# A 16-bit output product, ScalarE norms and an x tile taken ahead in a Mamba sandwich kernel

## The chip, the cores and the metric

The kernel runs on one core of one Trainium2 chip, whose engines TensorE, VectorE, ScalarE, GpSimd and SyncE run side by side, each in the order of its own queue. The metric is the device time of one launch in microseconds (us), lower is better.

## The reference

The input is 8 batches of 1024 tokens by 256 features, all float32. Every batch passes a state-space layer and a feed-forward layer, each between a layer norm of its input and one of its output, with the input added:

```python
x = x + _layernorm(mamba(_layernorm(x)))
x = x + _layernorm(ffn(_layernorm(x)))
# mamba: INNER = 512, 8 heads of 64, state 64
x = silu(causal_conv(inp @ Wx.T))            # 4 taps
z = inp @ Wz.T
b, c = x @ Wb.T, x @ Wc.T                    # per head
dt = softplus(x @ Wdt.T + b_dt)
state = exp(dt * a) * state + (dt * b) outer x ;  y = c . state   # over tokens
y = y + d_param * x
yn = group norm of y per head, over ALL tokens and 64 channels
out = (yn * silu(z)) @ Wout.T
# ffn: 1024 hidden, weights alpha * sign(w), exact gelu
```

The group norm needs the sums over all 1024 tokens of a batch before any of its output can be normalised, gated and multiplied by Wout.

## The kernel before

**Tiles.** A batch is two blocks (j = 0, 1) of 512 tokens, a block four chunks (q) of 128 tokens. Channels lie on partitions for the x, z, B and C projections (four tiles c of 128 channels by 512 tokens), tokens on partitions for the norms, Wout and the last feed-forward product. Projections run as three f16 products of high and low halves (split_product, L1429); a low half is what rounding to f16 left (x_low L1076, hidden_split L1283). The Wout product (attention_out, L1594) is f32, four products of 256 columns for each 128 tokens, each seen as two records.

**Order of the work.** turn_steps writes one list of steps for a batch, by hand. Every engine walks the same list and does its own part of each step, strictly in that order. Steps of kind "own" belong to batch b, "tail" to batch b-1 (its group norm, Wout, middle norm, feed-forward and end norm), "next" to batch b+1. So the tail of one batch is woven into the next. opening_steps stands before the first batch, and last_tail holds the tail of the last one, which nothing covers.

A block goes: head (x projected, convolved over its taps on VectorE at L1071, silu, high and low halves; z; in block 0 the group norm's end and the gate, and the tail's Wout product), B, dt, middle norm, C with the feed-forward's hidden tiles, then the chunk stage. In it, chunk q has a front (segment exponentials on ScalarE, x and B turned by TensorE, x times dt on VectorE L1175, its weighted form on GpSimd L788), a score (TensorE L1541, masked by VectorE L1184), ends (the decays at the chunk's ends: TensorE L1530, ScalarE exponential L991, times C on GpSimd L795), a carry (state products L1555 and L1564; GpSimd scales the state L806, VectorE adds L1190) and a back (TensorE L1577, VectorE adds into y, L1200). Woven in are the tail's second output product (O), its end statistics and root, end_norm and end_add, and for the following block in_stat, in_norm and the two transposes xT.

The end of the chunk stage, in the list before:

```python
steps += own(("front", j, 2)) + tail(("end_stat", j))
steps += own(("score", j, 2), ("carry", j, 1), ("ends", j, 2)) + tail(("end_root", j)) + own(("back", j, 1), ("head_stat", j, 0))
steps += own(("front", j, 3), ("score", j, 3)) + [(who, "xT", nj, 0)] + tail(("end_norm", j, 0))
steps += own(("carry", j, 2), ("ends", j, 3), ("back", j, 2)) + [(who, "silu_table"), (who, "xT", nj, 1)] + tail(("end_norm", j, 1))
steps += own(("carry", j, 3), ("back", j, 3))
```

**Norms.** statistics (L1033 to L1040) runs on VectorE, the inverse root on GpSimd (L740), and the norm itself, (v - mean) * root, on VectorE (normal, L1046) for all four norms: in, mid, ff, end. The input norm writes xn, which TensorE turns at L1439.

**Banks.** PSUM's eight banks are three rings: five for "own" products, two for the tail's, one for xT, cums and sums. A product waits (empty) until the product that was five back in its ring has been read; the x projection's tiles 1, 2 and 3 so wait for the readers of the last chunk's state and y products. The group-norm mean is one small product (L1584), its root is on GpSimd (L746), and ScalarE normalises (L999) what VectorE (L1245, block 0) or GpSimd (L772, block 1) multiplies by the gate.

## Time and profile before

| what | value |
|---|---|
| median of 3 runs | 1340.73 us (1339.92 to 1341.39) |
| profiled execution | 1339.59 us |
| its span in the profile | 1337.9 us |
| TensorE busy | 1261.0 us (94%) |
| VectorE busy | 1053.6 us (79%) |
| ScalarE busy | 751.2 us (56%) |
| GpSimd busy | 450.9 us (34%) |
| mean busy share of the DMA engines, by hardware queue | 7.4% |

The span runs from the first instruction to the last. PE is TensorE, PEld its weight loads, DVE VectorE, ACT ScalarE, POOL GpSimd. A timeline row gives a start and a length in us from the span's start; the bracket is how long the engine was idle before it, and which instruction ended that. Back-to-back instructions overlap by up to 0.1 us in the records, so busy time over count says what one costs in a row.

### The profile page before, as it was taken

The page shows a single profiled execution, that of the slowest core. Times are in us where ns is not written, and L with a number is a line of the kernel's source. Part 1 is how long each engine was busy: PE and PEld are TensorE (multiplying, and loading weights), DVE is VectorE, ACT ScalarE, POOL GpSimd, SP SyncE. Part 2 cuts the span into 40 slices and gives each one's busy share as a digit, 9 for nine tenths or more (in the row PEclk, how much of TensorE's full clock was granted, in tenths as well). Part 3 has the DMA queues.
Part 4 walks back from the last instruction along what each step waited for, and adds up shares of the span by engine and source line. Part 5 has one row for each costly group of instructions (what it writes and reads, how often), then busy time and mean ns, then how long its engine had stood idle before and what let it go on. Part 6 is the DMA issues. An engine that isn't in the chain of part 4 may idle for free.

```text
span 1337.9 us, 27890 instructions
## 1 busy us (share of the span) xinstructions
PE 1261.0 (94%) x10616; PEld 810.2 (61%) x10616; DVE 1053.6 (79%) x2494; ACT 751.2 (56%) x1270; POOL 450.9 (34%) x527
## 2 busy tenths in 40 slices
PE   6898999999999999999999999999999999999775
PEld 3564657566565756656575665757566575766543
DVE  5585878879887897878888798878978789786675
ACT  5564674547654475555745567454856548455321
POOL 2030335133441533324342233514243153322523
PEclk9999999999999999999999999999999999999878
DMA  7010000101010010101001010000101000010000
GB/s 225 1 49 1 17 0 2 48 1 49 1 49 1 2 48 1 49 0 49 1 1 48 1 49 1 26 24 2 48 1 49 1 21 13 1 33 1 33 1 31
DMA packets 30564, 32.89 MB, mean 25 GB/s; under 512 B 1856, under 2 KB 28628, under 8 KB 30432
## 3 DMA queue, kind: packets, MB, share of 16 engines
q1 hardware_dynamic: 30432, 31.11, 7.4%
q8 instruction: 85, 1.39, 0.4%
q14 instruction: 47, 0.39, 0.1%
HBM read 22.72 MB, written 8.39 MB: 23 GB/s over the span
## 4 chain that ended last, share of the span: by engine, by line
PE 68%; DVE 22%; issue 4%; ACT 3%; POOL 3%; DVEq 0%; POOLq 0%; ACTq 0%
PE bank L1429 24%; PE bank L1622 8%; PE bank L1609 8%; DVE xs L1071 4%; PE bank L1594 4%; PE bank L1541 4%; PE bank L1577 4%; PE bank L1519 4%; PE bank L1511 3%; DVE un L1046 2%; PE bank L1439 2%; PE bank L1564 2%; PE bank L1555 2%; DVE stats_end L1033 2%; PE bank L1530 1%
## 5 line engine op out<-in xcount | busy, mean ns | idle before, releaser
L795 POOL TENSOR_TENSOR Cd<-Cd,CT 128x512 f32<-128x512 f32 x64 | 83.5, 1305 | 376.7 <-ACT Cd L991 376.7
L1429 PE MATMUL bank<-sh,WbT 128*128 128x512 f16 x768 | 174.7, 383 | 7.1 <-DVE sh L1076 7.1
L1429 PE MATMUL bank<-sh,WcT 128*128 128x512 f16 x768 | 175.9, 379 | 0.0
L1071 DVE SCALAR_TENSOR_TENSOR xs<-xi,vectors,xs 128x512 f32<-128x512 f32 x192 | 143.2, 750 | 17.6 <-ACT xs L898 13.3
L1429 PEld LDWEIGHTS bank<-sh,WbT 128*128 128x128 f16 x768 | 74.1, 98 | 94.9 <-DVE sh L1076 6.4
L981 ACT ACTIVATE mt<-bank 128x512 f32<-128x512 f32 x128 | 69.6, 599 | 108.0 <-PE bank L1511 108.0
L1594 PE MATMUL bank<-WoutT,yT 128*128 128x256 f32 x512 | 117.8, 387 | 11.8 <-DVE yT L1245 11.8
L1429 PEld LDWEIGHTS bank<-sh,WcT 128*128 128x128 f16 x768 | 75.0, 98 | 86.7
L1609 PE MATMUL bank<-uh,sign1T 128*128 128x512 f16 x512 | 122.9, 386 | 2.6 <-DVE uh L1272 2.6
L1013 ACT ACTIVATE hf<-bank,vectors,alpha 128x512 f32<-128x512 f32 x128 | 99.6, 778 | 40.1 <-PE bank L1609 29.3
L1622 PE MATMUL bank<-sign2T,hh 128*128 128x256 f16 x1024 | 119.4, 276 | 1.8 <-DVE hh L1283 1.8
L1594 PEld LDWEIGHTS bank<-WoutT,yT 128*128 128x128 f32 x512 | 97.6, 193 | 31.9 <-DVE yT L1245 18.2
L957 ACT ACTIVATE CT<-bank 128x512 f32<-128x512 f32 x64 | 38.1, 595 | 136.1 <-PE bank L1429 136.1
L1622 PEld LDWEIGHTS bank<-sign2T,hh 128*128 128x128 f16 x1024 | 99.9, 99 | 19.3 <-issue 4.3
L1281 DVE TENSOR_SCALAR hh<-hf 128x512 f16<-128x512 f32 x128 | 54.9, 429 | 59.0 <-ACT hf L1013 58.5
L1184 DVE TENSOR_TENSOR mt<-bank,mt 128x512 f32<-128x512 f32 x128 | 82.4, 685 | 14.3 <-PE bank L1541 13.8
L1283 DVE SCALAR_TENSOR_TENSOR hh<-hf,hh 128x512 f16<-128x512 f32 x128 | 88.6, 692 | 4.4
L740 POOL TENSOR_TENSOR rstd_mid<-var_eps_mid,power 128x4 f32<-128x4 f32 x16 | 16.2, 1013 | 222.9 <-DVE var_eps_mid L1040 222.9
L1429 PE MATMUL bank<-xh,WxT 128*128 128x512 f16 x384 | 88.6, 385 | 0.0
L991 ACT ACTIVATE Cd<-bank 128x512 f32<-128x512 f32 x64 | 38.2, 597 | 88.6 <-PE bank L1530 88.6
L1609 PEld LDWEIGHTS bank<-uh,sign1T 128*128 128x128 f16 x512 | 49.5, 99 | 62.0 <-issue 6.4
L1429 PE MATMUL bank<-xh,WzT 128*128 128x512 f16 x384 | 85.7, 379 | 0.0
(196 smaller groups left out, 2524.3 us busy)
## 6 DMA issues: line engine op xcount, KB each, us to landing
xt<-L_attn_input_tensor_dram SPq DMA_DIRECT2D x16, 512.0 KB, 5.1
u<-L_attn_input_tensor_dram SPq DMA_DIRECT2D x16, 512.0 KB, 4.0
out_dram<-u SPq DMA_DIRECT2D x16, 512.0 KB, 3.0
yT<-in_L_ffn_w_dram SPq DMA_DIRECT2D x2, 512.0 KB, 8.9
u<-in_L_ffn_w_dram SPq DMA_DIRECT2D x2, 512.0 KB, 9.2
BT<-in_L_attn_Wx_dram SPq DMA_DIRECT2D x1, 512.0 KB, 4.8
...
```

Of the source, the lines that this page charges most:

```text
L795: pool.tensor_tensor(Cd[n % 2][:, :, :], Cd[n % 2][:, :, :], CT[:, :, q * P:(q + 1) * P], ALU.mult)\
L981: nc.scalar.activation(mt[n % 2][:, g].rearrange("p c t -> p (c t)"), bank(t, ("seg", j, q, g))[:, :], ACT.Exp).then_inc(seg_exp.sem, 1)
L1013: nc.scalar.activation(hf[f % 2][:, :], bank(t, ("H", j, f))[:, :], ACT.Gelu, bias=b1_col[:, f:f + 1], scale=alpha1[:, f:f + 1]).then_inc( ...
L1071: nc.vector.scalar_tensor_tensor(out=xs[:, c, :], in0=xi[:, c, k:k + BLK], scalar=taps[:, c, k:k + 1], in1=xs[:, c, :], op0=ALU.mult, op1= ...
L1184: nc.vector.tensor_tensor(v, bank(t, ("S", j, q, g))[:, :], v, ALU.mult).then_inc(mt_out.sem, 1)
L1281: nc.vector.tensor_scalar(hh[0][:, f, :], hf[f % 2][:, :], SG, None, ALU.mult).then_inc(hh_hi.sem, 1)
L1283: nc.vector.scalar_tensor_tensor(out=hh[1][:, f, :], in0=hf[f % 2][:, :], scalar=SG, in1=hh[0][:, f, :], op0=ALU.mult, op1=ALU.subtract).t ...
L1429: mm = nc.tensor.matmul(bank(t, key)[:, :], w[i][:, k, cols(m)], v[h][:, k, :], start=(a == 0), stop=(a == len(terms) - 1))
L1519: mm = nc.tensor.transpose(bank(t, key)[:, cols(c)], src[:, c, cols(q)], ident[:, :])
L1594: mm = nc.tensor.matmul(bank(t, key)[:, (i % 2) * D:(i % 2 + 1) * D], yT[:, c, (j * NQ + i) * P:(j * NQ + i + 1) * P], WoutT[:, c, :], sta ...
L1609: mm = nc.tensor.matmul(bank(t, key)[:, :], sign1T[:, k, cols(f)], uh[i][:, k, :], start=(a == 0), stop=(a == len(terms) - 1))
L1622: mm = nc.tensor.matmul(bank(t, key)[:, (i % 2) * D:(i % 2 + 1) * D], hh[p][:, f, cols(i)], sign2T[:, f, :], start=(a == 0), stop=(a == le ...
```

## The change

- The Wout product of block 1 becomes three f16 products (high x high, low weight x high, high x low) of 256 columns. Its operands are made by ScalarE (gated_high) and VectorE (gated_low), in block 0's chunk stage, into the buffer of the feed-forward's hidden halves. The weight is split once. The statistics of the middle norm take an epsilon scaled alike.
- The input and the end norm move from VectorE to ScalarE, as Identity with a scale (the root) and a bias (minus mean times root, made by a tiny VectorE instruction, shift). The input norm is written over xt, and x of the next batch is loaded when TensorE has turned it. xn is gone.
- In the chunk stage both transposes of the next block's input, the end statistics, the end root and the head statistics get other places.
- In block 1's chunk stage the first x tile of the next batch is projected after the scores of chunk 3, in the ring of one bank, and convolved in a buffer of its own (ahead) between back 2 and carry 3; the silu is in the next head, whose order changes with it.

The diff's core, with its parts in their order:

```diff
@@ -163,10 +164,10 @@
             steps += own(("z_silu",))
         elif j == 0:
 
-            steps += own(("xi", 0, 0), ("xi", 0, 1), ("xi", 0, 2)) + tail(("head_stat", NJ - 1, 1), ("gn_sum",), ("gn_mean",))
-            steps += own(("xi", 0, 3), ("conv", 0, 0), ("silu", 0, 0), ("xs_hi", 0, 0)) + tail(("gn_root",))
-            steps += own(("conv", 0, 1, 0, 2), ("z", 0, 0)) + tail(("gn_fold",)) + own(("conv", 0, 1, 2, 3), ("z", 0, 1))
-            steps += tail(("gate", 0, 0)) + own(("xs", 0, 0), ("silu", 0, 1), ("xs_hi", 0, 1), ("conv", 0, 2))
+            steps += own(("silu", 0, 0), ("xs_hi", 0, 0), ("xi", 0, 1), ("xi", 0, 2), ("xi", 0, 3))
+            steps += tail(("head_stat", NJ - 1, 1), ("gn_sum",), ("gn_mean",)) + own(("conv", 0, 1, 0, 1)) + tail(("gn_root",))
+            steps += own(("conv", 0, 1, 1, 3), ("z", 0, 0)) + tail(("gn_fold",)) + own(("conv", 0, 2, 0, 1), ("z", 0, 1))
+            steps += tail(("gate", 0, 0)) + own(("xs", 0, 0), ("silu", 0, 1), ("xs_hi", 0, 1), ("conv", 0, 2, 1, 3))
             steps += own(("z", 0, 2), ("z", 0, 3)) + tail(("gate", 0, 1)) + own(("xs", 0, 1), ("conv", 0, 3))
             steps += tail(("Wo", 0, 0)) + own(*[("z_in", 0, c) for c in range(KI)])
             for c in (2, 3):
...
@@ -215,11 +216,15 @@
         steps += own(("score", j, 1))
         norm = [(who, "in_norm", nj)]
         steps += own(("carry", j, 0), ("ends", j, 1)) + (own(("back", j, 0)) + norm if first else norm + tail(("O", j, 1)) + own(("back", j, 0)))
-        steps += own(("front", j, 2)) + tail(("end_stat", j))
-        steps += own(("score", j, 2), ("carry", j, 1), ("ends", j, 2)) + tail(("end_root", j)) + own(("back", j, 1), ("head_stat", j, 0))
-        steps += own(("front", j, 3), ("score", j, 3)) + [(who, "xT", nj, 0)] + tail(("end_norm", j, 0))
-        steps += own(("carry", j, 2), ("ends", j, 3), ("back", j, 2)) + [(who, "silu_table"), (who, "xT", nj, 1)] + tail(("end_norm", j, 1))
-        steps += own(("carry", j, 3), ("back", j, 3))
+        steps += own(("front", j, 2)) + [(who, "xT", nj, 0)] + own(("score", j, 2), ("carry", j, 1), ("ends", j, 2))
+        steps += [(who, "xT", nj, 1)] + own(("back", j, 1)) + tail(("end_stat", j)) + own(("front", j, 3), ("score", j, 3)) + tail(("end_root", j))
+        steps += [(who, "xi", nj, 0)] if j else []
+        steps += own(("head_stat", 1, 0)) if j else []
+        steps += own(("carry", j, 2), ("ends", j, 3)) + tail(("end_norm", j, 0), ("end_norm", j, 1)) + own(("back", j, 2))
+        steps += tail(("gated", 1, 0)) if j == 0 else []
+        steps += [(who, "conv", nj, 0)] if j else []
+        steps += [(who, "silu_table")] + own(("carry", j, 3), ("back", j, 3)) + ([] if j else own(("head_stat", 0, 0)))
+        steps += tail(("gated", 1, 1)) if j == 0 else []
         if j == 0:
...
-    steps += [("Wo", 0, 0), ("Wo", 0, 1), ("mid_stat", 0), ("mid_norm", 0), ("ff_stat", 0), ("ff_norm", 0)]
+    steps += [("Wo", 0, 0), ("Wo", 0, 1), ("mid_stat", 0), ("gated", 1, 0), ("gated", 1, 1), ("mid_norm", 0), ("ff_stat", 0), ("ff_norm", 0)]
...
+        WoutT_parts = [sb(f"WoutT{i}", [P, KI, D], F16) for i in range(2)]
...
-        xn = sb("xn", [P, NQ, D])
...
+        yg = [[v[:, j * KI:(j + 1) * KI, :] for v in hh] for j in range(NJ)]
+        ahead = hh[1][:, 0:2, :].rearrange("p a n -> p (a n)").bitcast(F32)
...
-            (tail_keys if who == "tail" else in_keys if kind in ("xT", "cums", "sums") else own_keys).extend(uses(kind, *at))
-        in_keys.sort(key=lambda key: (key[1], ("xT", "cums", "sums").index(key[0]), key))
+            turned = kind in ("xT", "cums", "sums") or (kind, *at) == ("xi", 0, 0)
+            (tail_keys if who == "tail" else in_keys if turned else own_keys).extend(uses(kind, *at))
+        in_keys.sort(key=lambda key: (key[1], ("xT", "xi", "cums", "sums").index(key[0]), key))
...
+        def conv_sum(j, c):
+            return ahead if j == c == 0 else xs[:, c, :]
...
-                sp.wait_ge(*xn_made.count(t.ago(1), (j + 1) * NQ))
+                if not opening(t):
+                    sp.wait_ge(*full(t.ago(1), ("xT", j, KD - 1)))
...
+            def normal(w, v, t, j, i):
+                act.wait_ge(*ln_shifts[w].count(t, j + 1))
+                nc.scalar.activation(v[:, i, :], v[:, i, :], ACT.Identity, bias=ln_shift[w][:, i:i + 1],
+                                     scale=rstd[w][:, i:i + 1]).then_inc(normed[w].sem, 1)
+
+            def input_norm(t, j):
+                for i in range(NQ):
+                    normal("in", xt[j], t, j, i)
+
+            def end_norm(t, j, m=None):
+                for i in range(NQ) if m is None else range(2 * m, 2 * m + 2):
+                    normal("end", ffn_buffer(t, j), t, j, i)
...
-                if c == 0:
-
-                    act.wait_ge(*full(s, ("X", sj, NQ - 1)))
-                    act.wait_ge(*sh_lo.count(s, (sj + 1) * KI))
-                    act.wait_ge(*skip_out.count(s, (sj + 1) * KI))
-                nc.scalar.activation(xs[:, c, :], bank(t, ("xi", j, c))[:, :], ACT.Identity, bias=conv_bias[:, c:c + 1],
+                if j == c == 0:
+                    if not opening(t):
+                        act.wait_ge(*full(t.ago(2), ("O", NJ - 1, NQ // 2 - 1)))
+                elif c == (0 if j else 1):
+                    past_readers(t, j)
+                nc.scalar.activation(conv_sum(j, c), bank(t, ("xi", j, c))[:, :], ACT.Identity, bias=conv_bias[:, c:c + 1],
                                      scale=last_tap[:, c:c + 1]).then_inc(tap_out.sem, 1)
...
             def x_silu(t, j, c):
                 act.wait_ge(*conv_out.count(t, (j * KI + c + 1) * (TAPS - 1)))
-                nc.scalar.activation(xs[:, c, :], xs[:, c, :], ACT.Silu).then_inc(xs_out.sem, 1)
+                if j == c == 0:
+                    past_readers(t, j)
+                nc.scalar.activation(xs[:, c, :], conv_sum(j, c), ACT.Silu).then_inc(xs_out.sem, 1)
...
+            def gated_high(t, j, m):
+                s, sj = (t, 0) if ring_of(t, ("O", 0, 0)) is not final else (t.ago(1), NJ - 1)
+                act.wait_ge(*full(s, ("O", sj, NQ // 2 - 1)))
+                for c in range(2 * m, 2 * m + 2 if j else 0):
+                    act.wait_ge(*g_late.count(t, KI + c + 1))
+                    nc.scalar.activation(yg[j][0][:, c, :], yT[:, c, BLK:T], ACT.Copy, scale=SY).then_inc(yg_hi.sem, 1)
...
+            def shift(w):
+                def step(t, j, m=0):
+                    if m:
+                        return
+                    dve.wait_ge(*ln_rstd[w].count(t, j + 1))
+                    nc.vector.scalar_tensor_tensor(out=ln_shift[w][:, :], in0=moments[w][:, :, 0], scalar=-1.0,
+                                                   in1=rstd[w][:, :], op0=ALU.mult, op1=ALU.mult).then_inc(ln_shifts[w].sem, 1)
+                return step
...
+            def gated_low(t, j, m):
+                for c in range(2 * m, 2 * m + 2 if j else 0):
+                    dve.wait_ge(*yg_hi.count(t, c + 1))
+                    nc.vector.scalar_tensor_tensor(out=yg[j][1][:, c, :], in0=yT[:, c, BLK:T], scalar=SY, in1=yg[j][0][:, c, :],
+                                                   op0=ALU.mult, op1=ALU.subtract).then_inc(yg_lo.sem, 1)
...
+                    if t.b + t.d + 1 < NB:
+                        dve.wait_ge(*xs_out.count(t.ago(-1), j * KI + 1))
...
-                pe.wait_ge(*(g_late.count(t, (m + 1) * KI) if j else g_out.count(t, (m + 1) * KI)))
+                pe.wait_ge(*(yg_lo.count(t, KI) if j else g_out.count(t, (m + 1) * KI)))
                 pe.wait_ge(*empty(t, key))
-                for i in (2 * m, 2 * m + 1):
+                for i in (2 * m, 2 * m + 1) if j else ():
+                    terms = [(c, w, v) for c in range(KI) for w, v in ((0, 0), (1, 0), (0, 1))]
+                    for a, (c, w, v) in enumerate(terms):
+                        mm = nc.tensor.matmul(bank(t, key)[:, (i % 2) * D:(i % 2 + 1) * D], yg[j][v][:, c, cols(i)],
+                                              WoutT_parts[w][:, c, :], start=(a == 0), stop=(a == len(terms) - 1))
```

## Rows read from the trace of the kernel before

**Rows 1.** Windows, one batch: us, then busy time (records) of each engine, TensorE's clock.
```profile
604.00:761.36 157.36, 153.89 (x1325) 98.93 (x1321) 130.38 (x309) 92.42 (x156) 55.38 (x62) 1.00 0.07 21
```

**Rows 2.** Timeline, TensorE, block 1's chunks and next head: start, us, work [idle before <- releaser].
```profile
613.61 0.40 PE L1530 MATMUL bank<-of_target,end_mask 64*64 64x512 f16 x2 [0.68 <-DVE mt L1184]
...
617.48 0.66 PE L1439 MATMUL bank<-ident,xn 128*128 128x128 f32 x4
...
621.93 0.67 PE L1564 MATMUL bank<-Cd,state 64*64 64x128 f32 x16 [0.16 <-issue]
...
623.56 4.06 PE L1429 MATMUL bank<-xh,WxT 128*128 128x512 f16 x18
...
635.27 3.72 PE L1594 MATMUL bank<-WoutT,yT 128*128 128x256 f32 x16 [0.54 <-DVE yT L1245]
...
639.45 3.72 PE L1594 MATMUL bank<-WoutT,yT 128*128 128x256 f32 x16 [0.46 <-DVE yT L1245]
```

**Rows 3.** Timeline, TensorE, head of block 1.
```profile
703.82 5.35 PE L1429 MATMUL bank<-xh,WxT 128*128 128x512 f16 x24
...
714.19 7.07 PE L1594 MATMUL bank<-WoutT,yT 128*128 128x256 f32 x32
...
721.10 2.75 PE L1429 MATMUL bank<-sh,WbT 128*128 128x512 f16 x12
```

**Rows 4.** Timeline, VectorE, end statistics, middle statistics, convolutions and last low halves.
```profile
610.83 1.39 DVE L1033 BATCH_NORM_STATS2 stats_end<-y 128x6 f32<-128x256 f32 x4
...
644.20 1.42 DVE L1033 BATCH_NORM_STATS2 stats_mid<-bank 128x6 f32<-128x256 f32 x4
...
706.68 2.33 DVE L1071 SCALAR_TENSOR_TENSOR xs<-xi,vectors,xs 128x512 f32<-128x512 f32 x3 [1.23 <-ACT xs L898]
...
718.85 1.29 DVE L1076 SCALAR_TENSOR_TENSOR sh<-xs,sh 128x512 f16<-128x512 f32 x2 [0.62 <-ACT sh L931]
```

**Rows 5.** Groups of instructions by form: shapes, count | busy us, mean ns | idle before.
```profile
L1594 PE MATMUL bank<-WoutT,yT 128*128 128x256 f32 x512 | 117.8, 387 | 11.8 <-DVE yT L1245 11.8
...
L1622 PE MATMUL bank<-sign2T,hh 128*128 128x256 f16 x1024 | 119.4, 276 | 1.8 <-DVE hh L1283 1.8
...
L931 ACT ACTIVATE sh<-xs 128x512 f16<-128x512 f32 x64 | 39.1, 622 | 1.0
...
L1283 DVE SCALAR_TENSOR_TENSOR hh<-hf,hh 128x512 f16<-128x512 f32 x128 | 88.6, 692 | 4.4
...
L1046 DVE TENSOR_SCALAR y<-y,moments_end,rstd_end 128x256 f32<-128x256 f32 x60 | 36.7, 652 | 1.1 <-POOL rstd_end L740 1.1
...
L1046 DVE TENSOR_SCALAR xn<-xt,moments_in,rstd_in 128x256 f32<-128x256 f32 x64 | 32.3, 564 | 1.2 <-POOL rstd_in L740 1.2
...
L999 ACT ACTIVATE yT<-yT,gn_shift,gn_scale 128x256 f32<-128x256 f32 x128 | 65.1, 586 | 14.4 <-DVE gn_shift L1238 14.4
...
L1234 DVE TENSOR_TENSOR gn_scale<-gn_rstd,vectors 128x4 f32<-128x4 f32 x8 | 1.3, 162 | 2.0 <-POOL gn_rstd L746 1.1
...
L870 ACT ACT_TABLE_LOAD x30 | 38.5, 1283 | 0.5
```

**Rows 6.** Timeline, GpSimd: two group-norm roots, and chunks 2 and 3 of block 1.
```profile
473.23 1.47 POOL L746 TENSOR_TENSOR gn_rstd<-gn_var,power 128x4 f32<-128x4 f32 x1 [4.45 <-DVE gn_var L1229]
...
615.97 1.01 POOL L740 TENSOR_TENSOR rstd_end<-var_eps_end,power 128x4 f32<-128x4 f32 x1
...
617.64 1.04 POOL L788 TENSOR_TENSOR xdw<-xdt,decays 128x512 f32<-128x512 f32 x1 [0.66 <-DVE xdt L1175]
...
619.46 0.61 POOL L806 TENSOR_TENSOR state<-state,decays 128x256 f32<-128x256 f32 x1 [0.77 <-PE bank L1564]
...
620.26 1.41 POOL L795 TENSOR_TENSOR Cd<-Cd,CT 128x512 f32<-128x512 f32 x1 [0.19 <-ACT Cd L991]
...
630.60 1.47 POOL L746 TENSOR_TENSOR gn_rstd<-gn_var,power 128x4 f32<-128x4 f32 x1 [4.45 <-DVE gn_var L1229]
```

**Rows 7.** Timeline, VectorE, middle norm after the last batch.
```profile
1273.92 1.90 DVE L1046 TENSOR_SCALAR un<-bank,moments_mid,rstd_mid 128x256 f32<-128x256 f32 x4 [1.20 <-POOL rstd_mid L740]
```

68 lines of the change are left out of this document (39 added, 29 removed).

## The prediction

> **What bounds the kernel now.** I read the page first (TensorE 94% busy), then one batch by windows, then TensorE's timeline for its gaps, then the other engines' timelines beside those gaps. One batch lasts 157.37 us, from one group-norm root on GpSimd to the next (473.23 to 630.60) [rows 6], and in a stretch of that length TensorE works in all but 3.5 us [rows 1], at the full 2.4 GHz. The gaps sit in two places. In the chunk stage of either block TensorE waits 0.68 us for VectorE's masked scores before the ends of chunk 2, and 0.16 us for the decayed C of chunk 3 [rows 2]. In the head of block 0 it waits for the gated output before each half of the output product (0.54 and 0.46 us) [rows 2]. The head of block 1 has no gap: the two projections and the output product run through and the B projection follows [rows 3]. So TensorE is the bound, but VectorE's chain is close behind: its last low half in block 1 is ready at 720.14 us and B's last quarter wants it at 721.10 + 1.95 = 723.05 us, a slack of 2.9 us [rows 3, 4].
>
> **The 16-bit product.** Block 1's output product is 32 records of f32 now and becomes 48 of f16. The f32 ones take 117.8/512 = 0.230 us each, f16 ones of the same 256 columns 119.4/1024 = 0.117 us [rows 5]; by the stretch of block 1, 6.9 us become 48 x 0.109 = 5.2 us. TensorE is offered 1.7 us per batch, 13.8 us over eight. For it ScalarE makes four high halves (39.1/64 = 0.61 us each) and VectorE four low halves (0.69 us each) per batch [rows 5]. The Trainium skill, Perfetto Trace Analysis, Identifying the Most-Contended Engine, says to work on the engine with the highest occupancy first. By that rule the sum would be these 13.8 us and the time some 1326 us; the windows show whether the other engines let it through, and that is a rival below.
>
> **The norms.** VectorE loses eight end norms of 36.7/60 = 0.61 us and eight input norms of 0.50 us a batch, 8.9 us; it gains the four low halves, 2.8 us, and four tiny shifts of 0.16 us [rows 5]. ScalarE takes 16 norms at 65.1/128 = 0.51 us [rows 5], and has gaps for the input ones. The price beside other work is nothing; if ScalarE were late there, the transposes would be late by as much. x is loaded in place and freed by TensorE instead of VectorE, some 8 us later in SP's queue, tens of us before its use: nothing.
>
> **The chunk stage, both blocks.** I go through block 1's; block 0's is the same 80.26 us later.
> - End statistics leave the place before chunk 2's masked scores, so the 0.68 us gap goes; both transposes of x (0.6 us each) move ahead of it. Chunk 3's scores end at 617.48 - 0.68 + 1.2 = 618.0 us.
> - The statistics (2.04 us, from 610.83) now stand before chunk 3's x·dt on VectorE: begun at 616.2, done 618.2, x·dt 618.9.
> - GpSimd's queue is then: weighted x·dt 1.04, end root 1.01, state scaling 0.61, decayed C 1.3 [rows 6]. Before, the root ran in a gap ahead of x·dt; now it stands before the state and the decayed C. I take 1.3 for the last (1.41 in its row, where VectorE adds beside it). These end at 618.9 + 1.04 + 1.01 + 0.61 + 1.3 = 622.9, and TensorE's state product of chunk 3 follows at 623.1 (0.26 us after GpSimd's end, as at 620.26 + 1.41 to 621.93) instead of 621.93.
> - So chunk 3's last product ends at 624.7 instead of 623.56: +1.2 us. In block 1 TensorE meanwhile did the first x tile of the next batch, 6 of 0.216 = 1.3 us, so there this is level. In block 0 it is a loss of 1.2 us.
>
> **Head of block 0, behind block 1's chunks.** The tile convolved ahead takes VectorE 3 x 0.75 us ahead of the last carry, which then ends at 625.4. The second x tile uses the bank that this carry reads, so TensorE waits 0.75 us, and has all x tiles at 629.4, as before [rows 2]. But the head has one convolution less. The group-norm root starts at 630.2 instead of 630.60, the product's first half at 634.9 instead of 635.27, and its second half follows without the 0.46 us, so B starts some 0.8 us earlier; middle statistics start at 642.9 instead of 644.20 [rows 2, 4, 6]. The chain to the next transposes moves by the same 0.8. **-0.8 us per batch, seven batches: -5.6.**
>
> **Head of block 1, behind block 0's chunks.** Here the low halves bite. ScalarE's end norms wait for the shift, which stands behind chunk 2's carry (622.2), last 2.1 us, and then come two high halves to 625.3, the table load, two more to 627.9. VectorE does two low halves before the last carry, then back 3, then the head statistics that were done earlier before, then the other two, until 629.7. The first convolution of block 1 starts there, against 706.68 - 80.26 = 626.4 before: +3.2 us. From it to the last low half VectorE needs the 13.4 us it needs now, so 723.3 us [rows 4]. TensorE, 1.2 later and 1.7 shorter, comes to B at 720.6 and meets the low halves one by one; B's first tile ends at 724.1 against 723.7. **+0.45 us per batch, seven: +3.2.** The 16-bit product is worth 0.8 of its 1.7 us here, since VectorE sets the end.
>
> **Once.** Batch 0 has no tail to hide chunk 3's decayed C: +0.6. Two more weight conversions on each of two engines: +0.3 (0 to 1). After the last batch VectorE's four low halves (2.8 us) stand before the middle norm, which waits 1.2 us for its root anyway [rows 7]: +1.5; the end norms wait for a shift: +0.4. **+2.8.**
>
> **Sum** -5.6 + 3.2 + 2.8 = +0.4 us on 1339.59 us, the profiled execution's own time, which is 1.1 us under the median of the runs. **1340.0 us**. Both heads are chains of some 20 steps over four engines, placed to 0.5 us at best; I allow 4 us about the sum.
>
> **Rivals.**
> - **The offer goes through (faster).** VectorE has 5.5 us a batch less to do and is not late in block 1: low halves or head statistics fall into waits that I counted twice. If its first convolution is less than 2 us later, TensorE's own times hold: -0.5 us with the 1.2 us wait for decayed C, -1.7 us without. That gives 7 x (-0.5 to -1.7) - 5.6 + 2.8 = -6.3 to -14.7: 1325 to 1333 us, say 1330. For it: VectorE is idle for 1.2 us before that convolution and ScalarE works only in 92 of 157 us [rows 1]. Against: the order in the queue is fixed, and each low half waits for ScalarE. What the page's rule of the most-contended engine gives lies at this end.
> - **The low halves hold block 1 (slower).** The place is VectorE's queue between chunk 2 and the first convolution of block 1. It decides from 3 us of delay: behind that, each us is a us per batch. If the last two low halves also wait for ScalarE's table load and the last carry, the delay is 4.8 instead of 3.2 us: +1.6 x 7 = +11, 1351 us. For it: the slack was 2.9 and the carry that the state needs is in the same queue. Against: those waits mostly overlap in my table.
> - **The norms reload ScalarE's table.** They stand among exponentials, where the rows show no Identity. A load of 1.3 us [rows 5] before the high halves delays the same chain: +1.3 x 7 = +9, 1349 us. Copies there cause none, so this is unlikely. ScalarE: Activation LUTs, of the Trainium skill (Table sets: the hidden batching unit), says cheap functions are in every set; no row shows Identity beside an exponential.
>
> **Numbers.** Forecast 0.40, offer goes through 0.30, low halves hold 0.26, reload 0.04. A measurement here tells about 0.2% (2.7 us) from no change. The forecast's own range is 1336 to 1344: 0.11 faster, 0.23 same, 0.06 slower. Altogether faster 0.41, same 0.23, slower 0.36. Both signs hold most of the chance, so the range reaches into both, 1328 to 1352 us.
>
> **What would show it.** Right: no gap before the ends of chunk 2; a gap of 0.7 us (block 1) and over 1 us (block 0) before chunk 3's state product, with GpSimd as the releaser; the second x tile waiting on the state; waits of B in block 1 for the low halves of x; the middle statistics of block 0 over 1 us earlier. Wrong: a batch period below 156.5 or above 158.2 us against 157.37; block 1's B starting without a wait; a table load inside the chunk stage.

## The result, and the profile after

| | before | after |
|---|---|---|
| median of 4 runs each | 1340.33 us | 1363.47 us |
| ratio, 95% interval | | 1.0173 (1.0154 to 1.0193) |
| profiled execution | 1339.59 us | 1363.99 us |
| TensorE busy | 1261.0 us (94%) | 1253.5 us (92%) |
| VectorE busy | 1053.6 us | 1039.2 us |
| ScalarE busy | 751.2 us | 831.6 us |

The kernel is 1.7% slower; 1340.0 us with a range of 1328 to 1352 was forecast. TensorE has 7.5 us less work and stands still longer. One period (group-norm root to group-norm root) as a window of the kernel after, columns as in [rows 1]:

```profile
621.00:780.50 159.50, 152.03 (x1331) 97.27 (x1330) 128.99 (x300) 102.29 (x177) 56.44 (x63) 1.00 0.06 21
```

A period takes 159.5 us instead of 157.37 with TensorE busy for 1.86 us less: it idles 7.5 us a batch, not 3.5. Where: its timeline in the same batch, block 1's chunks and next head, then block 0's chunks and block 1's head (bracket: idle before, releaser):

```profile
639.40 0.67 PE L1625 MATMUL bank<-Cd,state 64*64 64x128 f32 x16 [0.95 <-DVE yT L1254]
642.85 4.06 PE L1490 MATMUL bank<-xh,WxT 128*128 128x512 f16 x18 [1.76 <-DVE state L1244]
...
719.83 0.67 PE L1625 MATMUL bank<-Cd,state 64*64 64x128 f32 x16 [1.81 <-DVE yT L1254]
...
724.65 2.76 PE L1490 MATMUL bank<-xh,WxT 128*128 128x512 f16 x12 [0.44 <-DVE state L1244]
...
732.43 5.40 PE L1656 MATMUL bank<-WoutT,hh 128*128 128x256 f16 x48
...
739.27 0.82 PE L1490 MATMUL bank<-sh,WbT 128*128 128x512 f16 x3 [0.80 <-DVE sh L1130]
740.58 1.47 PE L1490 MATMUL bank<-sh,WbT 128*128 128x512 f16 x6 [0.49 <-DVE sh L1130]
```

The 0.68 us before the ends of chunk 2 and the two waits before block 0's output product [rows 2] are gone. In their place stand 0.95 and 1.81 us before chunk 3's state product, 1.76 and 0.44 us for the state ahead of the x tiles, and 1.29 us for the low halves of x at B. VectorE releases all of them. Its timeline in these two places:

```profile
634.22 0.69 DVE L1229 TENSOR_TENSOR xdt<-bank,dt_t 128x512 f32<-128x512 f32 x1
...
638.04 0.93 DVE L1109 SCALAR_TENSOR_TENSOR ln_shift_end<-moments_end,rstd_end 128x4 f32<-128x4 f32 x1
638.89 0.74 DVE L1254 TENSOR_TENSOR yT<-bank,yT 128x256 f32<-128x256 f32 x2
639.56 2.91 DVE L1125 SCALAR_TENSOR_TENSOR hh<-xi,vectors,hh 128x512 f32<-128x512 f32 x3
642.39 0.41 DVE L1244 TENSOR_TENSOR state<-state,bank 128x256 f32<-128x256 f32 x1
...
722.05 2.21 DVE L1304 SCALAR_TENSOR_TENSOR hh<-yT,hh 128x512 f16<-128x512 f32 x2 [2.00 <-ACT hh L1049]
724.18 0.41 DVE L1244 TENSOR_TENSOR state<-state,bank 128x256 f32<-128x256 f32 x1
...
726.49 1.27 DVE L1304 SCALAR_TENSOR_TENSOR hh<-yT,hh 128x512 f16<-128x512 f32 x2
727.68 2.32 DVE L1125 SCALAR_TENSOR_TENSOR xs<-xi,vectors,xs 128x512 f32<-128x512 f32 x3
```

The shift, four numbers a partition, takes 0.93 us, and the same work on two low halves takes 2.21 us at 722 and 1.27 at 726. The difference is what GpSimd does beside them (at 726 it is idle):

```profile
635.99 1.02 POOL L759 TENSOR_TENSOR rstd_end<-var_eps_end,power 128x4 f32<-128x4 f32 x1
636.98 0.61 POOL L825 TENSOR_TENSOR state<-state,decays 128x256 f32<-128x256 f32 x1
637.68 1.27 POOL L814 TENSOR_TENSOR Cd<-Cd,CT 128x512 f32<-128x512 f32 x1
640.17 0.61 POOL L825 TENSOR_TENSOR state<-state,decays 128x256 f32<-128x256 f32 x1 [1.23 <-PE bank L1625]
640.75 3.69 POOL L782 TENSOR_TENSOR u<-u,y 128x256 f32<-128x256 f32 x4
...
721.17 3.69 POOL L782 TENSOR_TENSOR u<-u,y 128x256 f32<-128x256 f32 x4
```

The whole account, by the starts of the group-norm roots on GpSimd: the first root starts at 169.21 instead of 158.53 us (+10.7), the next six periods take 957.1 instead of 944.5 us (+12.6), and the rest adds 1.0 (the seventh period 1.6 more, what follows it 0.6 less). That is 24.3 of the 24.4 us between the profiled executions. So there are two losses to explain: 2.1 us a batch, and batch 0.

### The profile page after: what moved, and what is told of

It is laid out like the page before. It is cut to its first block, busy times and chain, and to the rows that moved or that the text cites. A ratio compares the mean times of both kernels' runs of the same rounds, so it can differ in the third digit from the quotient of the medians.

```text
span 1362.2 us, 28268 instructions
## 1 busy us (share of the span) xinstructions
PE 1253.5 (92%) x10744; PEld 800.6 (59%) x10744; DVE 1039.2 (76%) x2432; ACT 831.6 (61%) x1432; POOL 458.4 (34%) x527
## 3 DMA queue, kind: packets, MB, share of 16 engines
q8 instruction: 86, 1.41, 0.4%
## 4 chain that ended last, share of the span: by engine, by line
PE 49%; DVE 19%; issue 14%; POOL 12%; ACT 5%; POOLq 0%; DVEq 0%; ACTq 0%
PE bank L1490 21%; PE bank L1675 8%; PE bank L1660 4%; PE bank L1688 4%; DVE xs L1125 4%; POOL Cd L814 3%; PE bank L1602 2%; POOL xdw L807 2%; DVE un L1097 2%; PE bank L1580 2%; DVE hh L1304 2%; DVE gn_stats L1261 1%; POOL state L825 1%; PE bank L1529 1%; POOL y L777 1%
## 5 line engine op out<-in xcount | busy, mean ns | idle before, releaser
L1490 PE MATMUL bank<-sh,WbT 128*128 128x512 f16 x768 | 177.8, 385 | 12.4 <-DVE sh L1130 12.4
L1125 DVE SCALAR_TENSOR_TENSOR xs<-xi,vectors,xs 128x512 f32<-128x512 f32 x168 | 125.2, 749 | 4.5 <-ACT xs L938 0.8
L807 POOL TENSOR_TENSOR xdw<-xdt,decays 128x512 f32<-128x512 f32 x64 | 66.7, 1042 | 71.5 <-DVE xdt L1229 71.5
L1602 PE MATMUL bank<-CT,BT 64*128 64x128 f32 x1024 | 75.0, 286 | 1.6 <-ACT mt L1023 1.6
```

The source lines that it names most:

```text
L807: pool.tensor_tensor(xdw[n % 2][:, :, :], xdt[n % 2][:, :, :], per_head(to_end[:, q, :]), ALU.mult)\
L1125: nc.vector.scalar_tensor_tensor(out=conv_sum(j, c), in0=xi[:, c, k:k + BLK], scalar=taps[:, c, k:k + 1], in1=conv_sum(j, c), op0=ALU.mult ...
L1490: mm = nc.tensor.matmul(bank(t, key)[:, :], w[i][:, k, cols(m)], v[h][:, k, :], start=(a == 0), stop=(a == len(terms) - 1))
L1602: mm = nc.tensor.matmul(bank(t, key)[:, cols(c)], BT[rows, c, cols(q)], CT[rows, c, cols(q)], start=True, stop=True)
```

## The experiments

All ratios are to the kernel before, run on the same chip. Medians of that kernel beside the experiments were 1339.4 to 1340.1 us. "Period" is the mean of the first six distances between group-norm roots in the profiled run.

**Which part costs what.** Four kernels take the three parts (16-bit product, ScalarE norms, order with the x tile ahead) apart.

p32, the changed kernel with its f32 product in block 1:

```diff
-        steps += tail(("gated", 1, 0)) if j == 0 else []
...
-        steps += tail(("gated", 1, 1)) if j == 0 else []
...
-                pe.wait_ge(*(yg_lo.count(t, KI) if j else ...
+                pe.wait_ge(*(g_late.count(t, (m + 1) * KI) if j else ...
```

> The changed kernel with its 16-bit product undone in block 1 (f32 weights and yT, no gated steps, the weights' 16-bit copies of the setup stay); order and ScalarE norms stay. Theory A (the steady loss of 2.15 us a batch is the price of VectorE's instructions in order at block 1's head: the four low halves and what stands before them push the convolutions by 4.6 us): without the low halves (0.69 to 2.21 us each beside GpSimd, 5.2 us in all) the second convolution of block 1's head comes near the kernel before's place again, the B tile's +1.85 us goes, the f32 product costs its 1.7 us more: the two cancel, the period stays 159.5 minus 0 to 0.8 us, the time 1357 to 1364 us. Rival B (the low halves are covered and the product's gain arrives; the loss lies in the new order alone): the period grows by the product's 1.7 us and the time to about 1375 us. Batch 0's +10.7 us stays under both, if it comes from the ScalarE norms and the clock.

Measured 1363.71 us, ratio 1.0185 (1.0162 to 1.0208), period 159.2, inside Theory A's range. The time does not tell it from the changed kernel (the intervals of the ratios overlap), so the product is worth nothing there within the noise. Its trace shows why: in the third period the waits at B are gone and the others stay, and five of its first six periods are 158.9 to 159.0 us, 0.55 less than in the changed kernel; the sixth has a stretch of lower clock and takes 160.6.

vnorm, the changed kernel with the norms on VectorE:

```diff
-                "weights": weights, "in_stat": input_stats, "in_norm": shift("in"), "xT": input_low,
+                "weights": weights, "in_stat": input_stats, "in_norm": norm_in_place("in"), "xT": input_low,
...
-                "end_stat": end_stats, "end_norm": shift("end")}
+                "end_stat": end_stats, "end_norm": norm_in_place("end")}
```

> The changed kernel with the two norms back on VectorE, in place (no shift, no ScalarE instruction for them); order and 16-bit product stay. Theory A (batch 0's +10.7 us comes from ScalarE: the norms stand behind 'back 0' in the first batch and xT0 waits for them, the table load stands ahead of the first norm; in the steady batches the norms on ScalarE cost little): batch 0 wins back most of it, 5 to 9 us, and the steady batches lose what VectorE gets: eight norms in each block, in a stretch in which VectorE has gaps: 0 to 0.8 us a batch, so 1355 to 1364 us. Rival B (ScalarE is where the steady loss comes from): the period falls from 159.5 towards 157.4 as well, and the time to about 1342 to 1348 us. Rival C (VectorE is the bound of the chunk stage in the new order): over 1372 us.

Measured 1369.31 us, 1.022 (1.0206 to 1.0234). Batch 0 came back (first root at 161.13 us), as Theory A has it, but the period is 160.8: the waits for back 2 before chunk 3's state product grow from 1.81 to 2.91 us (block 0) and from 0.95 to 2.05 us (block 1). Part of the loss is the clock: it falls in all of the first six periods but one, and that one takes 159.9 us, 0.4 more than the changed kernel's. That the time would stay under 1364 was wrong. Rival C's mechanism (VectorE has no room in the new order) is there, its bound of 1372 is not reached.

oldorder, the changed kernel with the steps of chunks 2 and 3 and of the head as before:

```diff
...
+        steps += own(("front", j, 3), ("score", j, 3)) + [(who, "xT", nj, 0)] + tail(("end_norm", j, 0))
+        steps += own(("carry", j, 2), ("ends", j, 3), ("back", j, 2)) + [(who, "silu_table"), (who, "xT", nj, 1)] + tail(("end_norm", j, 1))
...
+        steps += own(("carry", j, 3), ("back", j, 3))
...
```

> The changed kernel with the order of chunks and head as in the kernel before (no x tile ahead, transposes of the next x in chunk 3, both gated steps where they were: after the transposes' second turn and after back 3); 16-bit product and ScalarE norms stay. Theory A (the steady loss is the low halves plus the crowd that the new order makes at chunk 3's end: end root, shift of 0.93 to 1.03 us beside GpSimd, carry 3, state): the first gated pair still waits at the same place, the crowd goes: the period falls by about 1 us to 158.5, the time to 1352 to 1358 us; batch 0 keeps what is ScalarE's of its +10.7. Rival B (the low halves alone are the loss): no change, 1361 to 1366 us. Rival C (the order alone is the loss, the low halves are free and the product pays): period 156 us, 1335 to 1342 us.

Measured 1348.89 us, 1.0069 (1.0057 to 1.0082), period 157.3, first root still at 168.31: between Theory A and Rival C. The new order costs some 14 us (ratio 1.0173 against 1.0069), more than Theory A gave it; batch 0's loss is not in the order.

norms_only, the same with the f32 product:

> Of the change the ScalarE norms alone (and the setup's 16-bit weights): the order of before, the f32 product, in and end norms on ScalarE in place with a shift from VectorE. Against the kernel before (1340.3). Theory A (the norms cost batch 0 some 6 us through xT0's waits and little in the steady batches): 1343 to 1349 us, period 157.4. Rival B (ScalarE norms are the steady loss too): 159 us a batch, 1356 to 1362 us. Rival C (they free VectorE and pay): under 1338 us.

Measured 1356.58 us, 1.0125 (1.0111 to 1.0139): the norms alone cost 16.8 us. Batch 0 has 8.9 of it (first root at 167.47), and every period, 158.3 in five of six, has 1.0 more. Both of Theory A's figures were too low; the time lies in Rival B's range, the period between the two. ScalarE and TensorE in batch 0's chunk 2:

```profile
79.84 2.07 ACT L890 ACTIVATE xt<-xt,ln_shift_in,rstd_in 128x256 f32<-128x256 f32 x4 [1.41 <-DVE ln_shift_in L1100]
81.82 1.05 ACT L1014 ACTIVATE mt<-bank 128x512 f32<-128x512 f32 x2
```

```profile
82.54 1.26 PE L1591 MATMUL bank<-CT,BT 64*128 64x128 f32 x16 [2.31 <-ACT mt L1014]
83.73 1.12 PE L1605 MATMUL bank<-xdw,bt 128*64 128x64 f32 x16
```

ScalarE stood 1.41 us waiting for the shift and 2.07 in the norm, with the exponentials of chunk 2 queued behind both. TensorE idled 2.31 us, and then the granted clock fell, so that a product that takes 0.69 us at full speed took 1.12. The same comes again in block 1, with 2.21 us. In a steady batch the same happens in chunk 3:

```profile
711.71 1.09 ACT L890 ACTIVATE y<-y,ln_shift_end,rstd_end 128x256 f32<-128x256 f32 x2 [0.83 <-DVE ln_shift_end L1100]
712.71 0.57 ACT L1024 ACTIVATE Cd<-bank 128x512 f32<-128x512 f32 x1
```

```profile
714.88 0.67 PE L1614 MATMUL bank<-Cd,state 64*64 64x128 f32 x16 [0.99 <-POOL Cd L810]
```

**The 16-bit product where it does not meet the crowd.** product_only: the old order, VectorE norms (the input norm in place, which makes room for the weights), 16-bit product as in oldorder.

> Of the change the 16-bit product alone, in the order of before (gated steps after the next transposes and after back 3), input and end norms on VectorE (the input norm in place in the x tile, so that there is room for the 16-bit weights). With the f32 product and ScalarE norms the old order took 158.45 us a batch, with the 16-bit product and ScalarE norms 157.3. Theory A (the product pays in the old order, where it does not meet the new crowd at chunk 3's end, whoever does the norms): 157.4 minus 0.6 to 1.2 a batch, 1330 to 1336 us. Rival B (it pays only because ScalarE norms freed VectorE's time; with VectorE's norms the low halves find it full): 157.4 plus 0 to 1.5 a batch, 1340 to 1352 us.

Measured 1335.68 us, 0.9971 (0.996 to 0.9983), period 156.8, as Theory A said.

early: the same with the gated steps in block 0's hidden stage. Their former buffer is busy there, so the high halves go into un, and the low halves over yT.

```diff
         steps += own(("C", j, 2)) + tail(("H", j, 2), ("H", j, 3))
+        steps += tail(("gated", 1, 0)) if j == 0 else []
...
         steps += own(("C", j, 3)) + tail(("H", j, 4), ("H", j, 5))
+        steps += tail(("gated", 1, 1)) if j == 0 else []
```

> As product_only, but the gated steps stand in block 0's hidden stage (high halves into the tile un after its transposes, low halves in place over yT), where VectorE and ScalarE have gaps of 1.8 to 2.1 us in the trace of before. Theory A (what decides over the product's worth is where its low halves stand): the whole 1.7 us a batch and no wait at block 1's product: period 155.5 to 156, 1326 to 1331 us. Rival B (the product's gain is not in the low halves' place: the second block's head is held by something else, its convolutions): no better than product_only.

Measured **1328.39 us, 0.9926 (0.9911 to 0.994)**, period 156.1: 11 of the 13.8 us on offer, and the version that beats both kernels. The low halves at their new place take their own time, and the idle time before the next hidden tile shrinks from 2.10 us, before, to 0.90:

```profile
664.88 1.29 DVE L1301 SCALAR_TENSOR_TENSOR yT<-yT,un 128x512 f16<-128x512 f32 x2
667.07 0.43 DVE L1338 TENSOR_SCALAR hh<-hf 128x512 f16<-128x512 f32 x1 [0.90 <-ACT hf L1061]
...
669.20 1.28 DVE L1301 SCALAR_TENSOR_TENSOR yT<-yT,un 128x512 f16<-128x512 f32 x2
```

after_early: the changed kernel with only this move.

> The changed kernel with only this moved: the gated steps to block 0's hidden stage (as in early). Theory A (in the changed kernel the low halves in block 1's head hold its convolutions: its f32 form without them takes 158.94 us a batch): 158.9 minus 1.7 = 157.3 a batch, the time 1363.5 minus 8 times 2.2 = 1346 us, between 1343 and 1350. Rival B (the late carry, the shift and the convolution ahead hold block 1's head by themselves and the product finds cover nowhere): 158.9 to 159.5 a batch, 1358 to 1364 us.

Measured 1356.24 us, 1.0122 (1.01 to 1.0143), period 157.9, with five of six at 157.6 to 157.7. The low halves' place is worth 7 us, where 17 were expected; the time lies between Theory A and Rival B. Most of the steady loss of the new order is in chunk 3, where the gaps of 1.81, 0.95 and 1.75 us stayed. The profiled execution took 1352.25 us, near the low end of the five (1352.06 to 1359.27).

**Is it the length of the instructions or the order?** late_add leaves VectorE's queue alone. It moves GpSimd's addition at the end of block 0 into block 1's head and makes it wait there:

```diff
-            steps += tail(("Wo", 1, 0), ("Wo", 1, 1))
+            steps += tail(("end_add", 0), ("Wo", 1, 0), ("Wo", 1, 1))
...
-        steps += tail(("end_add", j))
+        steps += tail(("end_add", j)) if j else []
...
             def add_middle(t, j):
+                if j == 0 and not (isinstance(t.b, int) and t.b + t.d == NB - 1):
+                    pool.wait_ge(*sh_lo.count(t.ago(-1), 2 * KI))
```

> The changed kernel with only this moved: GpSimd's addition at the end of block 0 (four of 0.9 us beside VectorE's low halves and convolutions) waits until block 1's x tiles are split, out of the way. Theory A (the low halves take 2.21 and 1.21 us where they would take 0.69 each because GpSimd works beside them, and the convolutions too): block 1's head comes forward by 1.5 to 3 us, of which the second product's start takes 1 to 1.85: 7 times this, 1349 to 1357 us. Rival B (the length of those instructions decides nothing, the order in the queue does): 1361 to 1366 us. A later addition delays u and its store, which nobody waits for before the next batch's loads.

Measured 1359.99 us, 1.0151 (1.0135 to 1.0167), period 158.8. VectorE's group of low halves, by form, from 160 to 1270 us, in the changed kernel and then in late_add:

```profile
L1304 DVE SCALAR_TENSOR_TENSOR hh<-yT,hh 128x512 f16<-128x512 f32 x28 | 24.4, 909 | 14.0 <-ACT hh L1049 14.0
```

```profile
L1306 DVE SCALAR_TENSOR_TENSOR hh<-yT,hh 128x512 f16<-128x512 f32 x28 | 18.0, 683 | 14.0 <-ACT hh L1051 14.0
```

The same instructions at the same place in the queue fall from 909 to 683 ns when GpSimd is not adding beside them. So the stretching is shown, and by the traces it is worth 0.7 us a batch. The 1.5 us or more that Theory A wanted was too much: the time lies between its range and Rival B's, and it is not clear of the changed kernel's by the intervals of the two ratios.

**Repairs by place.** norms_moved takes norms_only and moves two steps:

```diff
-... (own(("back", j, 0)) + norm if first else norm + tail(("O", j, 1)) + own(("back", j, 0)))
+... (own(("back", j, 0)) if first else norm + tail(("O", j, 1)) + own(("back", j, 0)))
-        steps += own(("front", j, 2)) + tail(("end_stat", j))
+        steps += own(("front", j, 2)) + (norm if first else []) + tail(("end_stat", j))
-... [(who, "xT", nj, 0)] + tail(("end_norm", j, 0))
-... ("back", j, 2)) + [(who, "silu_table"), (who, "xT", nj, 1)] + ...
+... [(who, "xT", nj, 0)]
+... ("back", j, 2)) + tail(("end_norm", j, 0)) + [(who, "silu_table"), (who, "xT", nj, 1)] + ...
```

> As norms_only (1356.6 us: ScalarE norms in the order of before, f32 product), with two norm steps moved: in the first batch the input norm comes after front 2 (it stood after back 0 and before it), in all batches the first pair of the end norm comes after back 2 (it stood after the x transposes of chunk 3, before ends 3). Theory A (a norm on ScalarE costs nothing by its time but by what is queued behind it: in the first batch the exponentials of chunk 2 stood behind a wait for the shift and TensorE waited 2.31 us for them at a falling clock, twice; in the others the copy of Cd of chunk 3 stood behind the end norm, 0.99 us on TensorE): batch 0 wins back 6 to 9 of its 8.9 us and the period goes from 158.45 back to 157.4 to 157.7: 1338 to 1344 us. Rival B (the norms cost what ScalarE spends on them, wherever they stand): 1352 to 1357 us.

Measured 1367.18 us, 1.0201 (1.0188 to 1.0215): a miss on the total, right on batch 0 (first root at 159.85, 7.6 us earlier). The end norm's new place put the table load and the copy of the second transposes behind it, and TensorE paid there in both blocks:

```profile
719.20 2.98 PE L1479 MATMUL bank<-xh,WxT 128*128 128x512 f16 x13 [1.98 <-DVE xh L1106]
```

norms_after puts both pairs behind back 3, where ScalarE has nothing queued for 2.8 us:

```diff
         steps += own(("carry", j, 3), ("back", j, 3))
+        steps += tail(("end_norm", j, 0), ("end_norm", j, 1))
```

> As norms_moved, with both pairs of the end norm after back 3, where ScalarE's next work (the copies of xi) is 2.8 us away in the trace of before. Theory A (only what is queued behind a norm costs): the gap of 1.98 us before the x projections and the 0.99 before chunk 3's carry are both gone, period 157.3 to 157.6, 1339 to 1343 us. Rival B (the two-by-two norms, 2.07 us on ScalarE, now push xi's copies and with them the convolutions): 158.5 a batch or more, over 1348 us. What would show a gain from the freed VectorE: under 1336 us.

Measured 1342.15 us, 1.0024 (1.0014 to 1.0035), period 157.5, first root at 159.78. Between norms_only, norms_moved and norms_after the same instructions run on the same engines; 25 us lie in their places. norms_after fell as its Theory A said. best and best2 are norms_moved and norms_after with the product as in early:

> Order of before, 16-bit product with its gated steps in block 0's hidden stage, norms on ScalarE with the two steps moved as in norms_moved. early, with VectorE's norms, took 1328.4 us (156.06 a batch). Theory A (ScalarE norms at places where nothing is queued behind them are worth the little that VectorE's time is worth, since TensorE is the bound): 1326 to 1331 us. Rival B (the norms on ScalarE cost a wait somewhere in any place): 1333 to 1342 us. Rival C (VectorE's freed 8 norms a block pay): under 1325 us.

> norms_after with the 16-bit product and its gated steps in block 0's hidden stage: the old order, all three parts but the order. Theory A: early (1328.4 us) within 3 us: 1325 to 1331. Rival B as in norms_after: over 1336 us.

best: 1359.86 us, 1.0147 (1.0133 to 1.0161), with norms_moved's gap and a stretch of lower clock in five of its first six periods. best2: 1340.2 us, 1.0 (0.999 to 1.0011), period 156.7. Both missed Theory A; best lies outside all its ranges, best2 in Rival B's. Even well placed, the ScalarE norms take back what the product gives (early is 12 us faster). best2's profiled run took 1336.45 us, near the low end of its 11 (1336.23 to 1340.83), and shows only 0.7 us a batch of this; where the rest lies is open.

root_late, conv_late and all_late work on chunk 3 of after_early. root_late:

```diff
-        steps += [(who, "xT", nj, 1)] + own(("back", j, 1)) + tail(("end_stat", j)) + own(("front", j, 3), ("score", j, 3)) + tail(("end_root", j))
+        steps += [(who, "xT", nj, 1)] + own(("back", j, 1), ("front", j, 3), ("score", j, 3)) + tail(("end_stat", j))
-        steps += own(("carry", j, 2), ("ends", j, 3)) + tail(("end_norm", j, 0), ("end_norm", j, 1)) + own(("back", j, 2))
+        steps += own(("carry", j, 2), ("ends", j, 3)) + tail(("end_root", j)) + own(("back", j, 2)) + tail(("end_norm", j, 0), ("end_norm", j, 1))
```

> As after_early (the changed kernel without low halves in the head; 157.9 us a batch, 1356 us), with the tail's end norm put behind chunk 3's own work: statistics after score 3, root after ends 3, shift and norm after back 2. Theory A (in the changed order VectorE makes 2.3 us of statistics before xdt of chunk 3, GpSimd's root stands before state and Cd, and the shift, which waits for the root and takes 0.8 to 0.93 us, before back 2, whose bank TensorE waits for: 1.81 us in block 0, 0.95 in block 1): both gaps go, 1.5 to 2.7 us a batch: 1335 to 1345 us. Rival B (it is the late carry that holds TensorE and what follows takes the gap's place, or the later end norm delays the next hidden stage or u's store): 1352 to 1358 us.

Measured 1348.71 us, 1.0066 (1.0053 to 1.0078), period 157.2. 7.5 us came back, less than Theory A's least (11 us). The profiled executions are only 1.8 us apart, and the undisturbed periods (157.1 to 157.3 against 157.6 to 157.7) show 0.4 to 0.5 us a batch. The block 0 gap fell from 1.81 to 1.27 us, block 1's rose from 0.95 to 1.12, and the state's wait grew to 2.07. The trace shows what took the shift's place: the four end statistics now stand between score 3 and back 2 in VectorE's queue.

```profile
709.32 1.39 DVE L1088 BATCH_NORM_STATS2 stats_end<-y 128x6 f32<-128x256 f32 x4
...
711.75 0.74 DVE L1260 TENSOR_TENSOR yT<-bank,yT 128x256 f32<-128x256 f32 x2
```

conv_late moves only `(who, "conv", nj, 0)` behind back 3:

> As after_early, with only the convolution of the x tile projected ahead moved from before carry 3 to after back 3. Theory A (the 2.90 us of convolution before carry 3 hold the state, and with it TensorE, 1.76 us in block 1's end): the gap goes, but the convolution's SiLU comes 1.2 us later: 0.8 to 1.7 us a batch less: 1343 to 1350 us. Rival B (the head of the next batch waits for the first x tile's halves and takes the time back, so that projecting it ahead is worth what the gap costs): 1355 to 1358 us.

Measured 1366.49 us, 1.0209 (1.0195 to 1.0224). The gap before the x tiles fell from 1.75 to 0.28 us as Theory A said, and the time rose by 10 us, which neither said. Two things took the gain back. The first is Rival B's kind of wait: the convolution now stands ahead of the group-norm sums in VectorE's queue, and TensorE waits for these before the small product of the group-norm mean, where after_early has no wait of that size:

```profile
802.41 3.08 DVE L1130 SCALAR_TENSOR_TENSOR hh<-xi,vectors,hh 128x512 f32<-128x512 f32 x3
805.41 1.39 DVE L1266 BATCH_NORM_STATS2 gn_stats<-yT 128x6 f32<-128x256 f32 x4
```

```profile
808.10 0.39 PE L1650 MATMUL bank<-gn_mom,head_mean 128*128 128x8 f32 x2 [2.15 <-DVE gn_mom L1278]
```

TensorE's waits of over 0.3 us in the fourth period are 5.32 us in sum against 4.92, so the gap has moved and not gone. The second is the clock. Windows of 4 us around block 0's last chunk, conv_late and then after_early:

```profile
716.00:720.00 4.00, 3.44 (x72) 2.64 (x70) 2.37 (x9) 0.60 (x1) 2.83 (x4) 1.00 0.00 0
720.00:724.00 4.00, 2.55 (x33) 1.95 (x34) 2.59 (x7) 2.93 (x5) 2.78 (x4) 0.79 0.02 4
724.00:728.00 4.00, 4.00 (x16) 1.63 (x15) 2.01 (x6) 2.46 (x6) 1.57 (x3) 0.78 0.36 126
```

```profile
708.00:712.00 4.00, 3.24 (x70) 2.50 (x66) 2.37 (x6) 0.60 (x1) 3.03 (x4) 1.00 0.00 0
712.00:716.00 4.00, 2.75 (x38) 1.84 (x39) 2.74 (x8) 3.13 (x5) 2.78 (x5) 1.00 0.02 4
```

Both idle for about 1.8 us before the same product. In conv_late the granted clock then goes from 1.00 to 0.79 and 0.78 for two windows (4 x 0.21 + 4 x 0.22 = 1.7 us): of its two levels, 2.4 and 1.2 GHz, it is at the lower one for part of each. It falls so seven times between the first group-norm root and the last, four of them at this place and three about the new wait before the group-norm mean. In after_early it stays at 1.00 there in all batches but one. What decides between them the runs do not show.

all_late has root_late's statistics and root, end norm and convolution after back 3, and the first batch as in after_first:

> The changed kernel's order with the x tile ahead kept, and all that was late put right: low halves in block 0's hidden stage, statistics and root after chunk 3's score and ends, end norm and the convolution ahead after back 3, the first batch as in after_first. root_late took 1348.7 us with 2.07 us of waiting for the state and 1.27 and 1.12 for yT. Theory A (those gaps were the convolution and the shift in front of carry and back; the x tile ahead itself then costs nothing and gives up to 0.5 us a batch): 155.7 to 156.5 a batch, 1327 to 1335 us. Rival B (the x transposes' low halves in chunk 2 and 3 load VectorE where it has no room, whatever the order; the x tile ahead costs): 1336 to 1349 us.

Measured 1363.71 us, 1.0186 (1.0171 to 1.0201), a miss. The time is above both ranges. The state's gap is down to 0.27 us and those before chunk 3's state product stay as in root_late. In its place stands conv_late's wait, before the group-norm mean, with 2.35 us in the fourth period, and in five of its middle batches the clock falls there.

after_first, the changed kernel with the first batch's norm behind front 2 and its transposes after ends 2:

> The changed kernel with only the first batch changed: its ScalarE input norm after front 2 (the exponentials of chunk 2 no longer behind it), the x transposes of chunk 2 after ends 2. Theory A (10.7 us of batch 0 are that queue, the gap it leaves on TensorE and the lower clock that follows): batch 0 wins back 5 to 9 us, 1355 to 1359 us. Rival B (batch 0's loss is the opening's table load and the x tile ahead): 1361 to 1364 us.

Measured 1362.31 us, 1.0174 (1.016 to 1.0188), a miss of Theory A too: the first root is only 1.8 us earlier. The time lies in Rival B's range, but the trace does not show Rival B's cause. The exponentials were no longer late; the transposes' copies were, behind the norm instead:

```profile
84.92 0.66 PE L1500 MATMUL bank<-ident,xt 128*128 128x128 f32 x4 [1.41 <-DVE xh L1115]
```

**The x tile ahead by itself.** no_ahead is after_early without it; early_ahead is early with it.

> after_early (1356.2 us, 157.6 to 157.9 us a batch) without the x tile ahead: its projection, convolution and SiLU stand at block 0's head as in the kernel before; the chunk order (transposes in chunk 2, statistics, root and shift in chunk 3) stays. Theory A (the tile ahead puts 2.90 us of convolution before carry 3 and costs TensorE 1.76 us there, of which the head of block 0 gives back about 1 because its two waits of 0.5 us at the first product are gone): 0 to 0.8 us a batch less, 1350 to 1356 us. Rival B (the tile ahead pays, and the whole of the new order's cost is the crowded chunk 3): 0.3 to 1.5 us a batch more, 1358 to 1368 us.

> early (1328.4 us, 156.06 a batch: old chunk order, VectorE norms, 16-bit product with its gated steps in block 0's hidden stage) with the next batch's first x tile projected after the second transposes of chunk 3 and convolved after back 3. Theory A (the tile ahead pays where nothing is crowded: it takes away the head's waits of 0.55 and 0.46 us before the first product, and nothing is put ahead of a carry): 0.3 to 1.0 us a batch less: 1321 to 1327 us. Rival B (xi ahead stands before carry 3 on TensorE, and the head's first convolution is no earlier than it was, for want of the last transposes): 1328 to 1332 us, no difference. Rival C (the extra step before the carry shifts the head and brings a dip of the clock once a batch, as in conv_late): over 1335 us.

no_ahead: 1362.7 us, 1.0174 (1.016 to 1.0188), so in the new order the tile is worth 6.5 us (Rival B). Its undisturbed periods are 158.0, 158.2 and 157.8 us against after_early's 157.6 to 157.7, so the tile itself gives 0.2 to 0.6 us a batch; the others of over 160 us have stretches of low clock. early_ahead: 1357.21 us, 1.0139 (1.0119 to 1.0159), 29 us slower than early. Rival C's bound held, and the clock does fall in five of the middle batches, but two waits that no expectation had come first. With the transposes still in chunk 3, TensorE waits for their low half with chunk 3's last carry queued behind; and with the convolution after back 3 it waits before the group-norm mean, as in conv_late:

```profile
787.70 1.46 PE L1494 MATMUL bank<-xh,WxT 128*128 128x512 f16 x6 [1.90 <-DVE xh L1119]
...
797.83 0.39 PE L1649 MATMUL bank<-gn_mom,head_mean 128*128 128x8 f32 x2 [2.09 <-DVE gn_mom L1277]
```

So in the old order the tile ahead meets late transposes. In the new order these are early, but the end statistics stand in chunk 3, and there the order loses more than the tile gains. Not run was the old order with the tile's convolution before carry 3, so early_ahead's 29 us, lower clock included, are the price of both waits together and not of the late transposes alone.

All together, in us:

| | f32 product | low halves in the chunk stage | in the hidden stage |
|---|---|---|---|
| old order, VectorE norms | 1339.8 (before) | 1335.7 | **1328.4** |
| old order, ScalarE norms as changed | 1356.6 | 1348.9 | |
| old order, ScalarE norms well placed | 1342.2 | | 1340.2 |
| new order, VectorE norms | | 1369.3 | |
| new order, ScalarE norms | 1363.7 | 1363.5 (after) | 1356.2 |

## Why the prediction was wrong

The price of the ScalarE norms was the step that failed most: forecast at nothing, measured at 16.8 us (norms_only, in the old order). Next to it, "Once" and the two heads were sized for instructions that stand alone: the queue behind the first batch's norm was not in the sum, nor what GpSimd's work adds to VectorE's instructions beside it. Part by part:

- **The 16-bit product.** Its size was right: the product takes 5.40 us (5.2 forecast), and where its low halves are covered it brings 1.4 of 1.7 us a batch (early). "Worth 0.8 of its 1.7 us here" was mis-sized: in the changed kernel it is worth 0 within the noise (p32), since the gain is waited for at B.
- **The norms.** The step that failed most: "The price beside other work is nothing". The prediction counted ScalarE's idle time and not the place in its queue. The runs put 16.8 us on it in the old order: 8.9 in batch 0, where the shift comes late, and 1.0 a batch where an end norm stands before Cd. It had even named what to check ("if ScalarE were late there, the transposes would be late by as much"), but for the transposes alone, and not for batch 0, whose list has back 0 before the norm.
- **The chunk stage.** Right in its sums. Less the 16.06 us by which the stretch came later, chunk 3's state product of block 1 stands at 639.40 - 16.06 = 623.34 us (623.1 forecast), and block 0's, less its 16.37 us, at 703.46 against 702.20 before: 1.26 later where 1.2 were forecast. Even the decayed C of block 1 ends where it was said to (637.68 + 1.27 - 16.06 = 622.89 against 622.9). The releaser was not right: TensorE waited last for VectorE's back 2, which stood behind the shift. But that is 0.2 us: with the forecast's 0.26 us between GpSimd's end and TensorE's start, the decayed C alone would have held it to 639.21 instead of 639.40.
- **Head of block 0.** "-0.8 us per batch" was +0.3 (16.37 - 16.06). The tile ahead takes 2.91 instead of 2.25 us and the shift 0.93 instead of 0.16, both with GpSimd beside them; carry 3 ends at 626.7 instead of 625.4, and TensorE waits 1.76 instead of 0.75 us.
- **Head of block 1.** "+3.2 us" of delay at the first convolution was +4.6 (727.68 - 16.37 = 711.31 against 706.68), and B's end +1.83 (740.58 + 1.47 - 16.37 = 725.68 against 723.85) instead of +0.45. The rival "low halves hold block 1" named the place and, with 4.8, nearly the size. Its cause, a wait for the table load, was not there; the first pair took 2.21 us beside GpSimd's addition where 1.38 was forecast, and the shift ahead of ScalarE's norms 0.80 instead of 0.16. These two are the 1.4 us that the forecast lacked. Over the seven periods -5.6 + 3.2 = -2.4 became 12.6 + 1.6 = +14.2.
- **Once.** "+2.8" was 10.7 - 0.6 = +10.1. Chunk 3's decayed C was as small as forecast (gaps of 0.75 and 0.76 us); the queue behind the input norm and the lower clock after it were not in the sum. From 90 to 125 us the granted clock is 0.85 instead of 0.95 (35 x 0.10 = 3.5 us), from 67 to 90 us 0.93 instead of 1.00 (1.6 us).
- **The rivals.** The reload of ScalarE's table did not happen: the chunk stage has one load, as before. "The offer goes through" did not either: the product pays most (11 of 13.8 us, early) without the other two parts and at a place with slack, and beside the ScalarE norms in the old order it is worth 7.7 us (oldorder against norms_only).
- **The range.** It ended at 1352 since each rival changed one term only; three terms were off on the same side at once.
